# A Mamba-and-MLP kernel: the MLP tiles' scale arithmetic regrouped, five products by C moved from GpSimd to VectorE

## The reference, cut to what matters

```python
x = x + tanh(g_xattn) * mamba(ctx_1024, layernorm(x))   # conv, softplus, scan over L=512, gate silu(z)
x = x + tanh(g_ffn)   * ffn(layernorm(x))

# mamba, per batch b (4), channel d (512), state n (16):
state = state * exp(dt*A) + (dt*u)*B        # along L = 512
y     = sum_n state * C                     # "product by C", then the sum over n

# ffn: bitlinear(v, w) = einsum(quant(rmsnorm(v)), ternary(w))
def rmsnorm(v): return v * rsqrt(mean(v*v, -1) + 1e-6)
def activation_quant(v):
    scale = 127.0 / clip(max(abs(v), -1), 1e-5, None)
    return clip(round(v * scale), -128, 127) / scale
h = silu(bitlinear(x, w1)) * bitlinear(x, w2)           # 2048 wide
out = bitlinear(h, w3)
```

## Time and profile before

| what | us |
|---|---|
| median of 3 runs | 656.55 (655.85 to 657.06) |
| the profiled execution | 656.29 |
| its span | 654.5 |
| VectorE (DVE) busy | 583.0 |
| GpSimd (POOL) busy | 588.2 |
| ScalarE (ACT) busy | 531.1 |
| TensorE (PE) busy | 485.0 |

### The profile page before, as it was taken

The page is one execution under the profiler, slowest core; times in us unless marked ns, Lnnn a source line. Parts: engine busy times, 40 slices in busy tenths (PEclk is TensorE's granted clock), DMA queues, the critical chain, the costliest instruction groups (busy, mean ns, idle before and its releaser), DMA issues.

```text
span 654.5 us, 7928 instructions
## 1 busy us (share of the span) xinstructions
PE 485.0 (74%) x2560; PEld 293.4 (45%) x2560; DVE 583.0 (89%) x772; ACT 531.1 (81%) x969; POOL 588.2 (90%) x289
## 2 busy tenths in 40 slices
PE   8798888995454767778558485877666778578887
PEld 3254534543452444545535353554444545355443
DVE  7779789997998899999899999989998999999655
ACT  6764776798999688978888798898999898886665
POOL 1499999999999999999999999999999999999321
PEclk9898999997785979999777899989989997888899
DMA  5597687489950100256500000046700000000001
GB/s 185 211 406 288 215 311 288 167 322 385 386 197 6 33 2 1 77 163 242 169 31 1 32 2 17 1 153 231 260 16 1 17 2 17 16 2 17 1 17 48
DMA packets 24473, 80.77 MB, mean 123 GB/s; under 512 B 2465, under 2 KB 5153, under 8 KB 21361
## 3 DMA queue, kind: packets, MB, share of 16 engines
q1 hardware_dynamic: 24432, 80.27, 33.5%
HBM read 72.53 MB, written 7.73 MB: 123 GB/s over the span
## 4 chain that ended last, share of the span: by engine, by line
DVE 41%; ACT 22%; PE 18%; issue 13%; DMA 5%; SPq 2%; POOL 0%; DVEq 0%; ACTq 0%; POOLq 0%
DVE hh L773 13%; DVE hh L770 8%; DVE room L1048 4%; ACT da L736 3%; DVE sm L1093 3%; DMA wq<-x 3%; PE bank_y L851 3%; ACT da L743 2%; DVE da L773 2%; PE bank_a L1020 2%; PE da L1211 2%; PE bank_b L1029 2%; PE bank_b L256 1%; ACT room L1041 1%; ACT gbuf L922 1%
## 5 line engine op out<-in xcount | busy, mean ns | idle before, releaser
L773 DVE TENSOR_TENSOR_SCAN hh<-da,hh 128x1024 f32<-128x1024 f32 x85 | 193.3, 2279 | 3.2 <-ACT da L743 3.0
L851 PE MATMUL bank_y<-ident,hh 128*128 128x128 f32 x1024 | 142.6, 288 | 11.3 <-POOL hh L818 9.5
L851 PEld LDWEIGHTS bank_y<-ident,hh 128*128 128x128 f32 x1024 | 127.1, 150 | 40.8 <-issue 16.8
L813 POOL TENSOR_TENSOR hh<-hh,cc 128x1024 f32<-128x1024 f32 x60 | 141.4, 2357 | 0.3 <-ACT hl L756 0.3
L818 POOL TENSOR_TENSOR hh<-hh,cc 128x1024 f32<-128x1024 f32 x57 | 135.0, 2369 | 0.0
L708 POOL TENSOR_TENSOR hh<-pair,bb 128x1024 f32<-128x1024 f32 x30 | 71.0, 2366 | 24.9 <-DMA bb<-xd_scratch 23.3
L770 DVE TENSOR_TENSOR_SCAN hh<-da,hl,hh 128x256 f32<-128x256 f32 x128 | 85.3, 728 | 0.0
L708 POOL TENSOR_TENSOR hh<-wq,bb 128x1024 f32<-128x1024 f32 x32 | 75.7, 2373 | 2.0 <-PE bank_y L851 2.0
L702 POOL TENSOR_TENSOR hh<-wq,bb 128x1024 f32<-128x1024 f32 x32 | 75.4, 2355 | 0.2
L702 POOL TENSOR_TENSOR hh<-pair,bb 128x1024 f32<-128x1024 f32 x32 | 75.4, 2360 | 0.0
L736 ACT ACTIVATE da<-wq,cst 128x256 f32<-128x256 f32 x128 | 53.3, 462 | 11.9 <-DVE hh L770 11.6
(11 more groups left out here) (271 smaller groups left out, 1051.5 us busy)
## 6 DMA issues: line engine op xcount, KB each, us to landing
bb<-xd_scratch SPq DMA_DIRECT2D x32, 512.0 KB, 5.2
cc<-xd_scratch SPq DMA_DIRECT2D x32, 512.0 KB, 6.8
wq<-weights SPq DMA_DIRECT2D x12, 1024.0 KB, 6.2
stage<-weights SPq DMA_DIRECT2D x8, 1024.0 KB, 5.2
xin<-x SPq DMA_DIRECT2D x4, 1024.0 KB, 5.4
room<-weights SPq DMA_DIRECT2D x4, 1024.0 KB, 7.5
u_scratch<-wq SPq DMA_DIRECT2D x6, 512.0 KB, 2.9
wq<-x SPq DMA_DIRECT2D x2, 1024.0 KB, 18.5
```

The source lines that it names most:

```text
L773: ins = v.tensor_tensor_scan(to, da, h, 0.0, ALU.mult, ALU.add)
L813: ins = g_.tensor_tensor(quarters(flat(hh[k % NH])), quarters(flat(hh[k % NH])), cc[:, n:n + 4, t], ALU.mult)
L851: mm = pe.matmul(bank_y[:, (first + c) * P:(first + c + 1) * P], flat(hh[k % NH])[:, at:at + P], ident[:, :], start=False, stop=(s == STEP ...
```

## The change

- BY_VECTOR gains five steps: 42, 58, 84, 100, 109. Their products by C are done by VectorE.
- The peak of tiles 0 to 12 is one reduction over 2048 values at T+4; the reduction at T+2 and the joining of two peaks go.
- The squares of tiles 0 to 12 are one ScalarE operation over 2048 values at T+4 (its unused result in bf16 over the same space), with one small operation behind it.
- `rh_pool` moves from T+7 to T+6 (for tile 12 from the tail into slot 124).
- The scales: ScalarE makes rk = rh*kk at T+6; VectorE at T+7 makes hm = max(peak*rk, 1e-5), its reciprocal, and csh = 127*rk/hm, each waiting for the one before; ScalarE makes fin = hm*g3d behind its rounding at T+7. Part 0 at T+5 and the four operations at T+7 go.
- For a step that VectorE multiplies, `keep_state` stands ahead of the next exp in the slots from 80 on, since that exp overwrites the bank.

```diff
-BY_VECTOR = (14, 16, 25, 45, 49, 53, 62, 67, 68, 73, 77)
+BY_VECTOR = (14, 16, 25, 42, 45, 49, 53, 58, 62, 67, 68, 73, 77, 84, 100, 109)
...
+        def square_scalar(act, i):
+            act.wait_ge(*MV.of(("h", i, NCH - 1)))
+            MA.did(act.activation(view(room, 4096, 1024).bitcast(BF16), h_all(i), ACT.Square,
+                                  accum_out=ssq[:, 0:1]), ("sq", i))
             act.wait_ge(*MA.now())
+            act.wait_ge(*MA.of(("k2", rows_by(i))))
+            mean_square(act, i, 0, True)
...
+        def peak_vector(v, i):
+            v.wait_ge(*MV.of(("h", i, NCH - 1)))
+            MV.did(v.tensor_reduce(am1, h_all(i), AX.X, ALU.max, apply_absolute_value=True), ("peak", i))
...
+        def rk_scalar(act, i):
+            act.wait_ge(*MG.of(("rh", i)))
+            MA.did(act.activation(rk, rh, ACT.Copy, scale=kk[:, i % NE:i % NE + 1]), ("rk", i))
+
+        def scale_vector(v, i):
+            v.wait_ge(*MV.of(("peak", i)))
+            v.wait_ge(*MA.of(("rk", i)))
+            MV.did(v.tensor_scalar(hm, am1, rk, 1e-5, ALU.mult, ALU.max), ("hm", i))
+            v.wait_ge(*MV.now())
+            MV.did(v.reciprocal(hinv, hm))
+            v.wait_ge(*MV.now())
+            MV.did(v.tensor_scalar(csh, hinv, rk, 127.0, ALU.mult, ALU.mult), ("csh", i))
+
+        def fin_scalar(act, i):
+            act.wait_ge(*MV.of(("hm", i)))
+            MA.did(act.activation(fin[i % 2], hm, ACT.Copy, scale=g3d), ("fin", i))
...
@@ gpsimd
-                        if k == tile_slot(i) + 7:
+                        if k == tile_slot(i) + 6:
                             rh_pool(g_, i)
...
@@ scalar, k in 80..124 (fin_scalar, square_scalar and rk_scalar alike in 38..79)
+                    if c_by_vector(k + LEAD - 2):
+                        keep_state(act, k + LEAD - 2)
                     if k + LEAD < ALL:
                         exp(act, k + LEAD)
-                    if k + LEAD - 2 < ALL:
+                    if k + LEAD - 2 < ALL and not c_by_vector(k + LEAD - 2):
                         keep_state(act, k + LEAD - 2)
...
                             hq_scalar(act, i, 0)
                             hq_scalar(act, i, 1)
+                            fin_scalar(act, i)
...
-                        if k == tile_slot(i) + 2 or k == tile_slot(i) + 4:
-                            square_scalar(act, i, k - tile_slot(i) - 1)
+                        if k == tile_slot(i) + 4:
+                            square_scalar(act, i)
+                    for i in range(END):
+                        if k == tile_slot(i) + 6:
+                            rk_scalar(act, i)
...
@@ vector
                         if k == tile_slot(i) + 7:
-                            scales_vector(v, i, 1)
+                            scale_vector(v, i)
...
-                    for i in range(END):
-                        if k == tile_slot(i) + 5:
-                            scales_vector(v, i, 0)
                     for i in range(END):
                         if k == tile_slot(i) + 4:
-                            peak_vector(v, i, 1)
+                            peak_vector(v, i)
...
-                        if k == tile_slot(i) + 2:
-                            peak_vector(v, i, 0)
```

More of the change, by code:

```diff
@@ L120, in build @@
         dtw, xpw = sb("dtw", [P, DM]), sb("xpw", [P, NE, ROWS])
-        sm = sb("sm", [P, 282])
+        sm = sb("sm", [P, 285])
         ident16 = sb("ident16", [P, P], F16)
@@ L174, in build @@
         gates = cst[:, 92:94]
-        col = iter(range(282))
+        col = iter(range(285))
         def small(n=1):
@@ L193, in build @@
         ssq, ssv, amh = [small(3) for _ in range(3)]
-        am1, ram1, rh, rk_most, rk_am, csh = [small() for _ in range(6)]
+        am1, ram1, rh, rk, rk_most, rk_am, hm, hinv, csh = [small() for _ in range(9)]
         fin = [small() for _ in range(2)]
@@ L1054, in gated_vector, with h_all @@
             MV.did(v.tensor_tensor(h_at(i)[:, c, :], th[c % 2], b_[:, :], ALU.mult), ("h", i, c))
[L1056 to L1060, removed]
+        def h_all(i):
+            return h_at(i).rearrange("p a b -> p (a b)")
+        def square_scalar(act, i):
+            act.wait_ge(*MV.of(("h", i, NCH - 1)))
+            MA.did(act.activation(view(room, 4096, 1024).bitcast(BF16), h_all(i), ACT.Square,
+                                  accum_out=ssq[:, 0:1]), ("sq", i))
             act.wait_ge(*MA.now())
-            if c == 1:
-                act.wait_ge(*MA.of(("k2", rows_by(i))))
-            mean_square(act, i, c // 2, c == 3)
+            act.wait_ge(*MA.of(("k2", rows_by(i))))
+            mean_square(act, i, 0, True)
         def mean_square(act, i, j, last):
@@ L1089, in peak_end @@
                    ("peak", i, c))
[L1091 to L1094, removed]
+        def peak_vector(v, i):
+            v.wait_ge(*MV.of(("h", i, NCH - 1)))
+            MV.did(v.tensor_reduce(am1, h_all(i), AX.X, ALU.max, apply_absolute_value=True), ("peak", i))
         def v2_at(i):
-            return ssv[:, 2:3] if at_end(i) else ssv[:, 1:2]
+            return ssv[:, 2:3] if at_end(i) else ssv[:, 0:1]
+        def rk_scalar(act, i):
[12 more added lines that the diff above has]
+            MA.did(act.activation(fin[i % 2], hm, ACT.Copy, scale=g3d), ("fin", i))
         def scales_vector(v, i, part):
@@ L1101, in scales_vector @@
             if part == 0:
[L1102 to L1106, removed]
+                v.wait_ge(*MV.of(("peak", i, NCH - 1)))
+                MV.did(v.tensor_scalar(am1, amh[:, 0:1], amh[:, 1:2], amh[:, 2:3], ALU.max, ALU.max))
                 v.wait_ge(*MV.now())
@@ L1217, in out_vector @@
             v.wait_ge(*MP.of(("o", i)))
+            if not at_end(i):
+                v.wait_ge(*MA.of(("fin", i)))
             MV.did(v.scalar_tensor_tensor(out=x2_at(i), in0=bank_g(i)[:, :], scalar=fin[i % 2], in1=x2_at(i),
@@ L1426, in _ @@
                 times_c(g_, 125)
-                rh_pool(g_, 12)
                 times_c(g_, 126)
@@ L1607, in _ @@
                 hq_scalar(act, 12, 0)
+                fin_scalar(act, 12)
                 tanh_scalar(act, 13, 1)
@@ L1950, in _ @@
                         times_c_vector(v, k + LEAD - 1)
-                scales_vector(v, 12, 1)
+                scale_vector(v, 12)
                 gated_vector(v, 13, 0)
```

## The result

The changed kernel is slower: 661.61 us median of 5 runs (660.15 to 661.9) against 656.55; ratio 1.0061, 95% interval 1.0039 to 1.0082. Timed again in another comparison it was at 1.0039 (1.0019 to 1.0059). I had forecast 653.8, with 658.0 as the upper end of the wider range. The profiled execution has a span of 659.8 us instead of 654.5.

The account below looks back on a forecast made before the run. VectorE's work plus its waits was taken as the bound: work -1.4, GpSimd's lateness -1.1 and -0.8, handshake +0.5, sum -2.8 us, giving 653.8 us median. Own range 651.5 to 655.2; 8 in 10 within 649.8 to 658.0.

Parts of the forecast that it names:

- The bound: Stretch 200 to 604 us: VectorE's work plus waits sets the loop's length; GpSimd is full, not late.
- Scales and peaks: VectorE, tiles 0 to 12: new scale operations save 7.1 us (3.6 to 9.5), single peak reductions 0.6 (0 to 1).
- Five products: Five products by C moved to VectorE add 6.3 us there (5.7 to 7), including longer scans ahead of them.
- GpSimd's lateness: Tile 3, T+7: VectorE's wait for the power goes, -1.1 us; TensorE's 4.96 us wait for a product goes, -0.8.
- nothing gained, but moved: ScalarE: 2.92 us a tile against 2.8; T+2 loses 1.46, T+4 gains 0.86, covered by VectorE's longer peak: 0.
- Handshake: VectorE's hm waits for ScalarE's rk, which waits for GpSimd's rh: +0.5 us in all, 0 to 4.
- Tail: After scan(127): the small chain is a draw and the tail moves as VectorE does, 0 of its own.
- It comes out even: Rival, chance 0.26: VectorE's savings fall where it waits for ScalarE, -7.7 shrinks to about -5; change 0, 656.5 us.
- The slower rival: Longer square at T+4 delays gate branch and exp(T+9), with the handshake at its upper end: +2.8, 659.3 us; chance 0.20.
- The hidden bound: Rival, chance 0.12: GpSimd's products delay VectorE's tanh waits through TensorE; relief gives up to -10.7, 645.8 us, half 650.

Follow-up runs that it names:

- Scales alone: Changed kernel with the eleven products by C of the kernel before, so none of the five added; 1.0012 (0.9992 to 1.0031) against the kernel before.
- the second profile of before: The kernel before run once more, unchanged, for a second profile; stretch from scan(40) to scan(127) 395.8 us against 395.2.
- products alone: Kernel before with the five more products on VectorE and keep_state ahead of the exp for them, old scales; 1.0063 (1.0039 to 1.0088).
- the second comparison: The changed kernel timed again, unchanged, against the kernel before; 1.0039 (1.0019 to 1.0059).
- two products: Changed kernel with two of the five products (58 and 100) instead of five, new scales; 1.0060 (1.0039 to 1.0080) against the kernel before.
- on neither: Changed kernel with squares and peaks of tiles 0 to 12 in halves again; 1.0097 (1.0072 to 1.0121) against the kernel before.
- on one side alone: Changed kernel with the square in two halves again (T+2 and T+4), single peak kept; 1.0159 (1.0122 to 1.0196) against the kernel before.

## Why the prediction was wrong, step by step

- **The bound.** "What VectorE gains or loses counts nearly in full" is the step that failed. The loss did count, the gain didn't. Scales alone: work -7.1 us as forecast (-7.7), of which 5.1 came back as waits; in time, 1.0012 is no gain at all. I had read 382.6 of 404 us busy and the chain's 41% as one bound for the whole stretch. It is a bound that changes hands inside each tile: ScalarE at the slot of the roundings (T+7, the next tile's T+1), the two side by side at the square and the peak, VectorE where a product without a wait behind it cost its own time. For the other slots no experiment says who is last.
- **Scales and peaks.** Forecast 0.55 us saved a tile, measured 0.49: the small operations took 0.60 a tile (7.2 us in the 12 tiles whose T+7 lies in the stretch), not 0.53. The reductions saved 1.0 us, not 0.6. Right in size. After, from hm to the first operation that doesn't need csh:

```profile
609.73 0.20 DVE L1108 TENSOR_SCALAR sm<-sm 128x1 f32<-128x1 f32 x1
609.96 0.16 DVE L1110 RECIPROCAL sm<-sm 128x1 f32<-128x1 f32 x1
610.16 0.21 DVE L1112 TENSOR_SCALAR sm<-sm 128x1 f32<-128x1 f32 x1
610.29 0.68 DVE L1054 TENSOR_TENSOR wq<-room,bank_b 128x512 f32<-128x512 f32 x1
```

  0.56 us at this place, where the earlier trace rows gave 0.53.
- **Five products.** 6.3 forecast; 5.7 for the products and 1.0 for the scans ahead of them, 6.7: right. Alone they cost 4.7 us net: forecast 6.3 - 1.9 = 4.4.
- **GpSimd's lateness.** With the old scales right in size (-1.5 of 1.9). In the changed kernel TensorE's 4.96 us wait was 4.72 still. The power there waited 0.78 us for the later square, and a product by B stood ahead of the product by C: the forecast's -0.8 did not come there. The softplus pair holds VectorE 2.0 us more instead of 0.8 less; the two halves of the change alone give +0.2 and -0.3. This interaction, with the 1.5 us by which the changed stretch exceeds the sum of its halves, I did not isolate, and the times don't show it: 1.0012 and 1.0063 together make 1.0075, the changed kernel has 1.0061 and 1.0039.
- **ScalarE "nothing gained, but moved".** Its sum was about right (2.68 us a tile, forecast 2.8), and I looked for the danger at T+4. There the longer peak did cover the longer square: the gate branch's waits went from 0.9 to 0. The 0.37 us of rk and fin at T+7, which I had priced as work and not as path, were the place.
- **Handshake.** One wait for rk, 1.08 us, at tile 8, and it took the place of 0.97 of the tanh wait behind (1.38 to 0.41): right within the 0.5.
- **Tail.** 0 forecast, -1.0 in this profile, +0.3 against the second profile of before: no effect shown.
- **The rivals.** "It comes out even" had the right mechanism, savings that fall where VectorE waits for ScalarE, with 7.7 shrinking to 5; it shrank to 2. The slower rival had the wrong place. The hidden bound is refuted: products alone cost VectorE 6.2 us of work and gave back 1.5.
- **A rival that I left open.** The changed kernel's granted clock of TensorE is lower: over its 17 executions the median is 0.892, beside 0.906 for the kernel before in the second comparison. Among the 95 executions of the kernel before the clock goes with the time: the 60 at 0.904 or more take 657.9 us on average (mean clock 0.908), the 35 below 659.4 (0.897). Which of the two follows from the other isn't shown, and no kernel here sets the clock by itself. So a part of the 2.5 to 5 us, by that slope and 0.014 of clock an estimated 2, may come by way of TensorE's clock. The traces speak for ScalarE at the second tanh, where it is busy without a gap; they don't decide it for the softplus pair, for whose input ScalarE waits on TensorE (2.17 us at 266.51 in the changed kernel, 0.97 at 262.86 before).

In the stretch: forecast -2.8, measured +4.2. Of the 7.0 between them 5.2 are the scales (-7.7 + 0.5 against -2.0), 0.3 the products, 1.5 the interaction.

## What to carry to other kernels

Where two engines hand a chain to each other in every slot, price an edit slot by slot: find who is last at each hand-over, and count an operation taken off the other one as nothing and one put on the last one as its whole start-to-start time. Work moved onto a saturated engine was nearly free in the slots where it waited, and elsewhere cost most of its own time (4.7 us in the stretch for 6.2 of work) or more (two products, 3.2 us for 2.4); look at the wait right behind the place, and at what the earlier engine will need there that the later one never had to wait for. Grouping two operations takes work out of one slot of each engine: here it did no harm on both sides of the pair or on neither, and cost another 0.6 to 1% on one side alone.

## What the runs showed of the hardware

VectorE's product with one operand in PSUM took 1.22 to 1.23 us at 228 of its 229 places in the 16 profiles (1.20 at one), always beside a busy GpSimd; beside an idle one it was never seen. GpSimd's product by C took 2.37 us on average, both with such a product of VectorE beside it (132 of them) and without one (1631): no blocking between them was seen. ScalarE's square of 2048 values with a bf16 result took 1.90 us on average, as much as the 1.905 of an operation over 2048 with an fp32 result. TensorE's mean granted clock was 0.894 in the changed kernel's profile and 0.908 in that of before; it was 0.889 to 0.912 over all profiles. Among the executions of the kernel before, those with a lower clock took longer (659.4 against 657.9 us on average, as above); which causes which isn't shown.
